# Routed experts in a 12-layer decoder on Trainium2: first product with the expert's matrix as weights, loaded for each tile

## What is computed

```python
# L1_ffn: softmax over the two largest logits; hidden 512, gated
h = jnp.einsum('nd,edh->enh', xf, W1) + b1[:, None, :]      # W1: 8 x 256 x 1024
a, g = jnp.split(h, 2, axis=-1)
act = jax.nn.silu(a) * g
out_e = jnp.einsum('enh,ehd->end', act, W2) + b2[:, None, :]
# L2_ffn: hidden 1024, not gated                             W1: 8 x 256 x 1024
h = jax.nn.gelu(jnp.einsum('td,edh->teh', flat_x, W1) + b1, approximate=False)
y = jnp.einsum('teh,ehd->ted', h, W2) + b2
```

## Time and profile before

| what | value |
|---|---|
| median of 3 runs | 3577.44 us (3577.3 to 3579.2) |
| profiled execution | 3583.66 us |
| its span, first to last instruction | 3581.9 us |
| mean granted clock of TensorE | 0.89 |
| HBM read, written | 102.54 MB, 23.43 MB |
| L1_ffn's tile loop in the span | 1719.8 to 1947.6 us |
| L2_ffn's tile loop in the span | 2634.4 to 2921.0 us |

### The profile page before, as it was taken

One profiled execution on the slowest core, in us unless ns is written; L12 is line 12 of the kernel. 1 busy time (PEld: TensorE's weight loads), 2 busy tenths in 40 slices (PEclk: granted clock), 3 DMA queues, 4 the chain that ended last, 5 costly groups with the idle time before them and its releaser, 6 DMA issues. The chain is left out here.

```text
span 3581.9 us, 56421 instructions
## 1 busy us (share of the span) xinstructions
PE 2857.3 (80%) x17461; PEld 1923.1 (54%) x17462; DVE 1611.4 (45%) x3767; ACT 1304.4 (36%) x3821; POOL 870.6 (24%) x556
## 2 busy tenths in 40 slices
PE   6545999687769899995797577888569956978798
PEld 3343677454545555552464245666347645856465
DVE  5776888604441333334343665555512226532311
ACT  1322777523431133331121215666313315822111
POOL 2343555300010222222101444444220024300000
PEclk8767999888879899996898688999679987989899
DMA  2000000000510100004111101000411110010000
GB/s 105 1 1 23 17 13 13 2 24 25 111 24 24 35 14 13 10 7 171 48 43 50 45 10 36 13 13 7 198 56 32 32 51 26 0 35 26 25 24 20
DMA packets 99899, 127.31 MB, mean 36 GB/s; under 512 B 56451, under 2 KB 84450, under 8 KB 96466
## 3 DMA queue, kind: packets, MB, share of 16 engines
q1 hardware_dynamic: 88898, 106.46, 9.4%
q0 software_dynamic: 6144, 14.69, 1.4%
q10 hardware_dynamic: 4752, 4.85, 0.4%
HBM read 102.54 MB, written 23.43 MB: 35 GB/s over the span
## 5 line engine op out<-in xcount | busy, mean ns | idle before, releaser
L1177 POOL TENSOR_TENSOR L_xattn_p<-L_xattn_p,L_xattn_ri 112x1500 f32<-112x1500 f32 (+1 forms) x192 | 436.0, 2271 | 651.7 <-DVE L_xattn_ri L1380 651.7
L1307 ACT ACTIVATE L_xattn_pT<-ps 125x448 f32<-125x448 f32 (+1 forms) x576 | 255.1, 477 | 383.1 <-PE ps L1227 382.5
L1319 ACT ACTIVATE L_xattn_p<-L_xattn_sa,L_xattn_ng 112x375 f32<-112x375 f32 x512 | 305.1, 599 | 67.5 <-DVE L_xattn_ng L1409 48.4
L1227 PEld LDWEIGHTS ps<-ident,L_xattn_p 112*125 112x125 f32 x1920 | 258.5, 190 | 87.8 <-issue 19.9
L1227 PE MATMUL ps<-ident,L_xattn_p 112*125 112x112 f32 x1920 | 283.5, 279 | 14.5 <-POOL L_xattn_p L1177 8.8
L268 PE MATMUL ps<-ident,ln_xn 112*128 112x112 f32 x416 | 98.9, 397 | 240.2 <-DVE ln_xn L237 221.7
L867 PE MATMUL ps<-L_ffn_weights,L_ffn_xsT 128*128 x560 | 256.1, 601 | 1.6 <-ACT L_ffn_xsT L910 1.1
L257 POOL TENSOR_TENSOR ln_rstd<-ln_tmp,ln_half 112x8 f32<-112x8 f32 x26 | 45.7, 1758 | 867.2 <-DVE ln_tmp L210 673.0
L1199 PE MATMUL ps<-L_xattn_pack,L_xattn_src 97*125 97x256 f32 (+3 forms) x576 | 198.2, 467 | 30.5 <-DVE L_xattn_v L1359 29.9
L1189 PE MATMUL ps<-L_xattn_src,L_xattn_pack 96*128 96x375 f32 x512 | 199.5, 515 | 25.3 <-DVE L_xattn_kT L1340 19.0
L268 PEld LDWEIGHTS ps<-ident,ln_xn 112*128 112x128 f32 x416 | 66.5, 210 | 273.2 <-issue 245.3
(11 more groups left out here) (378 smaller groups left out, 5357.4 us busy)
## 6 DMA issues: line engine op xcount, KB each, us to landing
L_xattn_src<-in_ctx SPq DMA_DIRECT2D x64, 281.2 KB, 2.9
L_ffn_weights<-in_L_ffn_experts SPq DMA_DIRECT2D x8, 2052.0 KB, 24.9
L_attn_toeplitz<-L_attn_h SPq DMA_DIRECT2D x4, 3136.0 KB, 23.7
L_ffn_weights<-in_L_ffn_experts SPq DMA_DIRECT2D x8, 1540.0 KB, 19.5
L_ffn_xs<-rows_in SPq DMA_DIRECT2D x74, 128.0 KB
rows_out<-L_ffn_y SPq DMA_DIRECT2D x70, 128.0 KB, 1.7
rows_in<-zeros ACTq DMA_DIRECT2D x1, 4736.0 KB, 27.4
L_ffn_w<-in_L_ffn_experts SPq DMA_DIRECT2D x4, 1026.0 KB, 5.0
```

What stands on the lines that cost most here:

```text
L1177: g.tensor_tensor(P[:, m % 4, :, :], P[:, m % 4, :, :], ri[:, m % 4, :].unsqueeze(2).broadcast_to([T, W, S2]), ALU.mult).then_inc(s["prob_ ...
L1227: last = pe.transpose(turned(t)[:, j * T:(j + 1) * T], P[:, m % 4, j, kc * KW:(kc + 1) * KW], k.ident[0:T, 0:T])
L1307: act.activation(PT[:, m % 4, kc, :, :].rearrange("p h t -> p (h t)"), turned(t), ACT.Copy).then_inc(s["pt_ev_a"].sem, 1)
L1319: last = act.activation(P[:, n % 4, j, :], at, ACT.Exp, bias=ng[:, n % 4, j:j + 1], scale=-1.0 if mask else 1.0, accum_out=rs[:, n % 4, j: ...
```

## The change

The first product takes the expert's w1 as the stationary operand, in 128 x 128 blocks, and xT as the moving one, 128 columns. Its result has the hidden features on partitions already, so `turn_hidden` and the DVE copies to hs go away, and ACT and DVE read its PSUM banks, now 2u and 2u + 1, directly. w1 is no longer resident: SP loads the expert's w1 for each tile from DRAM into one of two buffers, `load_first`, once the first product of two tiles before is done. The resident tile keeps w2 and b1 alone. `route.expert` gets two entries more, as the loads run two tiles past the end.

```diff
-def expert_tiles(k, route, name, weights, layout, rows_in, rows_out, hidden, gated, act_fn):
+def expert_tiles(k, route, name, weights, dram, layout, rows_in, rows_out, hidden, gated, act_fn):
...
-        hs = sb("hs", [KT, wide])
+        w1 = sb("w1", [KP, 2, 2, wide])
...
+                def load_first(t, u):
+                    e = expert(mybir.EngineType.SP, t)
+                    sp.wait_ge(*s["rg_up"].at(2 * t - 2))
+                    sp.dma_start(w1[:, u, :, :].rearrange("p c n -> p (c n)"),
+                                 dram[bass.ds(e, 1), :, 0:first_cols].rearrange("e p n -> (e p) n")).then_inc(
+                                     w_in[u].sem, 16)
+
...
-                load(0, 0)
-                load(1, 1)
+                for t in range(2):
+                    load(t, t)
+                    load_first(t, t)
                 sp.wait_ge(*s["rg_turned"].at(1))
                 load(2, 0)
+                load_first(2, 0)
                 with sp.Fori(0, NT // 2) as i:
                     for u in range(2):
                         t = 2 * i + u + 1
                         sp.wait_ge(*s["rg_turned"].at(t + 1))
                         load(t + 2, 1 - u)
+                        load_first(t + 2, 1 - u)
                         store(t - 1, u)
...
                 def first_product(t, u):
-                    e = expert(mybir.EngineType.PE, t)
                     pe.wait_ge(*s["rg_xT"].at(t + 1))
+                    pe.wait_ge(*w_in[u].at(8 * (t - u) + 16))
+                    pe.wait_ge(*s["rg_hT"].at(t - 1))
                     for half in range(2):
-                        pe.wait_ge(*s["rg_hs"].at(2 * t + half - 1))
-                        for c in range(2):
-                            last = pe.matmul(k.ps[:, half, 0:512], xT[:, u, c, :],
-                                             weights[:, bass.ds(e * total + (o1 + c * wide + half * 512), 512)],
-                                             start=(c == 0), stop=(c == 1))
+                        for j in range(4):
+                            at = half * 512 + j * KP
+                            for c in range(2):
+                                last = pe.matmul(k.ps[:, 2 * u + half, j * KT:(j + 1) * KT], w1[:, u, c, at:at + KP],
+                                                 xT[:, u, c, :], start=(c == 0), stop=(c == 1))
                         last.then_inc(s["rg_up"].sem, 1)
...
-                def turn_hidden(t, u):
-                    for half in range(2):
-                        pe.wait_ge(*s["rg_hs"].at(2 * t + half + 1))
...
                         first_product(t, 1 - u)
                         turn_tokens(t + 1, u)
                         second_product(t - 1, u)
-                        turn_hidden(t, 1 - u)
...
-                    act.wait_ge(*s["rg_ut"].at(2 * t + 1))
+                    act.wait_ge(*s["rg_up"].at(2 * t + 1))
...
-                                              k.ps[:, 2 + m // 4, (m % 4) * KT:(m % 4 + 1) * KT], act_fn,
-                                              bias=weights[:, bass.ds(e * total + (ob + m), 1)])
+                                              k.ps[:, 2 * u + m // 4, (m % 4) * KT:(m % 4 + 1) * KT], act_fn,
+                                              bias=weights[:, bass.ds(e * rest + (ob + m), 1)])
...
-                    v.wait_ge(*s["rg_ut"].at(2 * t))
-                    for half in range(2):
-                        v.wait_ge(*s["rg_up"].at(2 * t + half + 1))
-                        v.tensor_copy(hs[:, half * 512:(half + 1) * 512], k.ps[:, half, 0:512]).then_inc(
-                            s["rg_hs"].sem, 1)
...
     def load_experts(sp):
         for e in range(E):
-            sp.dma_start(weights[:, e * total:(e + 1) * total], edram[e, :, :]).then_inc(k["exp_in0"].sem, 16)
+            sp.dma_start(weights[:, e * rest:(e + 1) * rest], edram[e, :, first_cols:total]).then_inc(k["exp_in0"].sem, 16)
```

More of the change, by code:

```diff
@@ L667, in __init__ @@
         self.weight = k.tile(ctx, "weight", [T, PICKS, B], F32)
-        self.expert = k.tile(ctx, "expert", [1, self.tiles], mybir.dt.int32)
+        self.expert = k.tile(ctx, "expert", [1, self.tiles + 2], mybir.dt.int32)
 def place_tokens(k, route, gates, E, steps, turns):
@@ L687, in place_tokens @@
         ends, start = sb("ends", [T, 2, E]), sb("start", [T, E])
-        passed, owner = sb("passed", [1, route.tiles, E]), sb("owner", [1, route.tiles])
+        passed, owner = sb("passed", [1, route.tiles + 2, E]), sb("owner", [1, route.tiles + 2])
         pick = sb("pick", [T, PICKS, B])
@@ L766, in _ @@
                 ch.link(v.tensor_tensor(passed[:, :, :], turns[:, :, :],
-                                        ends[0:1, ea:ea + 1, :].broadcast_to([1, route.tiles, E]), ALU.is_ge))
+                                        ends[0:1, ea:ea + 1, :].broadcast_to([1, route.tiles + 2, E]), ALU.is_ge))
                 ch.link(v.tensor_reduce(owner[:, :], passed[:, :, :], AX.X, ALU.add))
@@ L787, in scatter_tokens @@
     return scatter
-def expert_tiles(k, route, name, weights, layout, rows_in, rows_out, hidden, gated, act_fn):
+def expert_tiles(k, route, name, weights, dram, layout, rows_in, rows_out, hidden, gated, act_fn):
     nc, s = k.nc, k.signals
     NT, total = route.tiles, layout["_total"]
[L798 to L802, removed]
+    wide = (2 if gated else 1) * hidden * KP
+    first_cols = 2 * wide
+    assert layout["w1"] == (0, KP, first_cols) and wide == 1024 and NT % 2 == 1
+    rest = total - first_cols
+    o2, ob = (layout[f][0] - first_cols for f in ("w2", "b1"))
     with ExitStack() as ctx:
@@ L877, in second_product @@
                         last = pe.matmul(k.ps[:, 6 + u, 0:D], hT[:, u, m, :],
-                                         weights[:, bass.ds(e * total + (o2 + m * D), D)],
+                                         weights[:, bass.ds(e * rest + (o2 + m * D), D)],
                                          start=(m == 0), stop=(m == hidden - 1))
                     last.then_inc(s["rg_down"].sem, 1)
-                def turn_hidden(t, u):
-                    for half in range(2):
-                        pe.wait_ge(*s["rg_hs"].at(2 * t + half + 1))
-                        pe.wait_ge(*s["rg_first" if gated and half == 0 else "rg_hT"].at(t))
-                        for j in range(4):
-                            last = pe.transpose(k.ps[:, 2 + half, j * KT:(j + 1) * KT],
-                                                hs[:, (half * 4 + j) * KP:(half * 4 + j + 1) * KP], k.ident[:, :])
-                        last.then_inc(s["rg_ut"].sem, 1)
                 turn_tokens(0, 0)
@@ L960, in expert_tiles @@
         k.advance(rg_in0=16 * ((NT + 3) // 2), rg_in1=16 * ((NT + 2) // 2), rg_out0=16 * ((NT + 1) // 2),
[L961 to L962 removed]
+                  rg_out1=16 * (NT // 2), rg_turned=NT + 1, rg_xT=NT + 1, rg_up=2 * NT, rg_w0=16 * ((NT + 3) // 2),
+                  rg_w1=16 * ((NT + 2) // 2), rg_hT=NT, rg_first=NT if gated else 0, rg_down=NT, rg_y=NT)
 def gather_results(k, route, name, rows):
@@ L1002, in sub_routed_ffn @@
     elay = dict(elay, _experts=E)
-    total = elay["_total"]
-    weights = k.tile(ctx, name + "_weights", [KP, E * total])
+    first_cols, total = elay["w1"][2], elay["_total"]
+    rest = total - first_cols
+    weights = k.tile(ctx, name + "_weights", [KP, E * rest])
     gates = k.tile(ctx, name + "_gates", [T, E * B])
@@ L1023, in sub_routed_ffn @@
     k.advance(exp_in0=16 * E)
-    expert_tiles(k, route, name, weights, elay, k.rows_in, k.rows_out, spec["hidden"], spec["gated"], spec["act"])
+    expert_tiles(k, route, name, weights, edram, elay, k.rows_in, k.rows_out, spec["hidden"], spec["gated"], spec["act"])
     gather_results(k, route, name, k.rows_out)
@@ L3198, in host_ffn @@
         small["steps"] = on_rows(np.tile(np.arange(N // KT, dtype=np.float32) * KT, 8))
-        small["turns"] = on_rows(np.repeat(np.arange(token_tiles(8), dtype=np.float32), 8), 1)
+        small["turns"] = on_rows(np.repeat(np.arange(token_tiles(8) + 2, dtype=np.float32), 8), 1)
     done = [packed(e) for e in experts]
```

16 lines of the change are left out of this document (8 added, 8 removed).

## The result

The changed kernel takes 3537.72 us (median of 4 runs, 3535.15 to 3543.13), beside 3578.32 (3577.3 to 3583.28) for the kernel before in the same comparison: a ratio of 0.9879, 95% interval 0.9867 to 0.9892, or 40.6 us less. The profiled execution took 3543.13 us (span 3541.4) where that of before took 3583.66 (span 3581.9).

What follows compares the result with a forecast made beforehand. TensorE (PE) was taken to bound both tile loops. Transposes gone -61, first products +10, starts +5 and ends -3 gave -49 us: 3528.6 us as the median, with 3519 to 3546 for 8 in 10.

Steps and rivals of the forecast that it cites:

- What goes: Both tile loops: eight hs transposes a tile leave PE, 0.87 us, 61 us in all; the DVE copies worth nothing.
- What comes on PE: First product of each tile: 32 instructions at 0.112 us, 3.58 us, 0.14 more than before.
- The rivals with slots of 0.14 and of 0.30: First product slower: weight loads hide less, 3591 us, chance 3%; or do not hide at all, 3948 us, 1%.
- The weight transfer: Both tile loops: 1024 KB a tile lands 5.0 us after issue, hidden behind PE's work; DMA share about 0.6.
- The slack of 2.3 us: L1_ffn: weights land 5.2 us after the first product's end and are wanted 7.5 us after it.
- the late-weights rivals: Tile loops wait for weights: late but still gaining, 3552 us, chance 10%; later still and slower, up to 3635 us, 3%.
- their landing of 8.5 us: First late-weights rival's example: with that landing L1_ffn turns in 6.19 us and gains 2 us instead of 25.
- Edges at the start: Start of each stage: tile 0's weights land 2.5 us late, twice, +5 us.
- its end of 4 each: Upper end of the forecast delay at each stage's start, 4 us; the lower end was 0.5.
- the 0.9 between token issue and weight issue: Start of each stage: tile 0's weights issued behind the tokens, after their issue and a 0.3 us register load.
- 0.73 was counted for each: Every tile in both stages gets 0.73 us shorter, 0.87 less 0.14; 70 tiles give 51 us.
- Edges at the end: Last wait before the final second product: 1.55 us saved in L1_ffn, 3.15 in L2_ffn; 0.7 and 2.3 of these extra.

Runs made afterwards that it cites:

- the idle ones: Changed kernel plus eight identity transposes, read by nobody, after each second product of the loop: 3596.86 us in one execution.
- no later loads: Changed kernel without its loads of w1 after tiles 0 and 1, whose weights serve the later tiles: 3538.67 us in one execution.
- old product: Changed kernel with streamed w1 kept, but the former first product, transposes and DVE copies of hs back: 3589.64 us in one execution.
- known expert: Changed kernel with the first two w1 loads of a stage fixed to expert 0, without a register load: 3529.22 us, ratio 0.9863.
- moved code: Changed kernel with 16 already met waits on SP in the empty block ahead of the tile loop: 3538.06 us, ratio 0.9869.
- early weights: Changed kernel with weights of tiles 0 and 1 issued one block earlier: first run 3524.61 us, ratio 0.9853; second 3522.7 us, ratio 0.9838.
- the store first: Changed kernel with SP storing y of t-1 before it issues the weights of t+2: 3569.07 us in one execution.

## Why the prediction was right, and what it got wrong

**The direction, the range and the mechanism were right**: 0.9879 is faster, and 3537.72 lies in the 3519 to 3546 given. It is 9 us above the 3528.6, of which 4 to 5 are in the change itself by the profiled pair (-44.6 for -49) and 0.9 in the median before, 3578.32 for 3577.44; the rest is no more than the medians are uncertain by, as the interval of the ratio runs from 38.6 to 47.6 us.

**What goes.** 61 us for the transposes: the idle ones cost the same 0.11 us each when put back. The DVE copies were costed at nothing; that was not tried alone, but DVE's busy time fell by 92 us and PE's turns are explained without it.

**What comes on PE.** 0.112 us a slot, taken from a run of four with the same columns, held for a run of 32 beside 238 GB/s of DMA writes: 3.57 for the forecast 3.58, and turns of 5.518 and 7.245 for 5.53 and 7.25. The rivals with slots of 0.14 and of 0.30 fall. 2240 weight loads of 128 rows, 0.195 us each in the mean, ran with matmuls 0.112 apart; by the rule in the Trainium skill, TensorE: Matmul & The Clock Gate, Part 3, such loads overlap with matmuls only when the row group differs. The trace disagrees, over the whole of both loops. The same part also says that a load into the background weight buffer is pulled ahead of matmuls; the trace fits that, but no run here shows the buffer.

**The weight transfer.** 5.1 us for 5.0 forecast; GB/s of 238 and 183 for 237 and 181; a share of 0.71 in L1_ffn for about 0.6, as the bytes were put at 411 GB/s for a share of 1, and the window gives 238 / 0.71 = 335. The slack of 2.3 us in L1_ffn is real and small: with the load issued 3.4 us later, or with twice the bytes, that stage loses 32 us while L2_ffn loses 2 to 3. So the late-weights rivals had the right place. The later issue amounts to their landing of 8.5 us, for which the first of them had a turn of 6.19; 6.52 was measured in the mean. The token rows behind the 1 MB were put at about 7 us, and landed in 2.2; they are issued 3.4 us behind a load that lands in 5.1, and 2.1 ahead of the next one, so they meet only its end.

**Edges at the start: the step that failed.** It said 2.5 us late, twice, from 0.9 us between token issue and weight issue and 5.0 of landing; measured 4.5 and 4.8, +9.3 for +5, outside its end of 4 each. The landing was right, 4.99 and 5.21. The term that failed is the 0.9 between token issue and weight issue: 2.75 and 2.82 us between their first packets. Where SP's pause is away from this place (no later loads, old product, known expert, moved code), the packets lie 0.5 to 1.1 apart and the starts are 3.6 to 4.7, that is 2.4 to 3.4 late, the forecast's 2.5 or somewhat over. The pause has a mark in the trace of the kernel before too, but it cost nothing there, and no row gave its price; the end of 4 was too near all the same.

A second part was left out altogether: the first two turns. The first gives back 0.38 us in L1_ffn and takes 0.05 in L2_ffn, and the second turn takes 0.51 and 0.68, where 0.73 was counted for each: 2.1 too little in all. Most of it is tile 0's first product, from its start to the next transposes: 5.39 and 5.46 us before, 6.57 and 6.21 after, for the forecast's 0.14 more. PE works at the lower clock there in both kernels, but longer in the changed one (in L1_ffn the granted clock over it is 0.65 and 0.53), where it stood idle just before, waiting for the weights.

**Edges at the end: better than forecast.** L1_ffn's last wait shrank by 1.1 for a forecast 1.55, L2_ffn's by 3.15 as forecast to 0.02. But the last second product of L1_ffn now takes 1.99 us, in place of 3.48 in the earlier trace rows, since the clock stayed at its upper level; the forecast had no such term, so this part is luck. The windows around it, of the kernel before and then of the changed one, show granted clocks of 0.61 and 1.00:

```profile
1943.50:1947.60 4.10, 3.48 (x8) 2.52 (x8) 0.42 (x1) 0.00 (x0) 0.00 (x0) 0.61 0.00 0
```

```profile
1926.90:1929.20 2.30, 1.99 (x8) 1.44 (x8) 0.13 (x2) 0.00 (x0) 0.00 (x0) 1.00 0.34 128
```

PE idled for 2.37 us ahead of it before, for 2.13 after. The shorter wait does not settle it: in the first run with early weights PE idled for the same 2.14 us, and the clock fell (0.73 from 1913.90 to 1916.70):

```profile
1913.98 2.62 PE L891 MATMUL ps<-L_ffn_weights,L_ffn_hT 128*128 x8 [2.14 <-DVE L_ffn_hT L950]
```

Of the nine traces with the new product and this wait of 2.1 us, seven show 1.99 for it, this one 2.62 and that with the store first 2.96.

Not tried: the new product on a w1 that stays resident, which would need no loads at all; and the DVE copies by themselves. Where SP's pause comes from stays open.

The sum in short, beside the forecast's -49: steady turns 0.5 better (-47.3); starts 4.3 worse; first turns 2.1 worse; ends 1.2 better; which gives the table's -44.4.

## What to carry to other kernels

When an fp32 product's result must be transposed afterwards, try the operands swapped: with 128 x 128 weights and 128 columns a slot took 0.112 us here, hardly more than half of the 0.215 of 256 columns, and the transposes are saved. When a matrix becomes a stream, count two things apart: whether a transfer fits into its slack at steady state (it did, by 2.3 us, and the order on the issuing queue decides it), and the first loads, which should be issued as soon as their address is known; hoisting two DMAs into the block before gave 11 to 12 us of layer time, a quarter on top of the change's own 44.6.

## What the hardware showed that was not expected

- SP paused for about 2 us at the entry of a block (one semaphore instruction of 1.4 us and 0.7 behind it), and edits of its program moved the pause or took it away. What it cost hung on what was issued behind it: nothing in the kernel before, 1.7 us a start in the changed one. Comparisons of a few us between kernels with different code on that queue should allow for it.
- Small transfers suffered most from a doubled load: at a share of 0.97 and 370 GB/s the first 1 MB landed in 5.3 us instead of 5.1, the 128 KB ones in 4.8 and 5.4 instead of 2.2 and 1.8. Whether the share did it or the place behind 2 MB on the queue is not separated: with the store first, at a share of 0.59, token rows issued 1 us behind the load took 4.4 us too.
- The granted clock had fallen after PE's idle gaps of 3.4 and 3.6 us ahead of the tile blocks, and after the 2.37 us at the end of L1_ffn before; over the 2.13 us at the same place after, it stayed up in most traces and fell in two. So a difference of 1 to 1.5 us at such a place can be that of two executions, and not the change's.
